# A graph layer pair on one core: shares in twos, chunk 5's sums in PSUM, edge bytes on ScalarE, eight tiles begun early

## The reference

```python
def _ggc(x, adj, W, wih, whh, bih, bhh):        # run twice, with relu around each
    m = adj @ (x @ W)
    gi, gh = m @ wih.T + bih, x @ whh.T + bhh
    r = sigmoid(i_r + h_r); z = sigmoid(i_z + h_z)
    n = tanh(i_n + r * h_n)
    return (1.0 - z) * n + z * x
x = layernorm(x + both gated layers)
# second layer: weights that depend on the rank of each edge in its row
support = x @ weight
mask = (adj != 0); rank = cumsum(mask, axis=1); deg = rank[:, -1:]
k = minimum(deg, 100); pos = rank - (deg - k)
w = mask * where(pos > 0, 0.5 ** (k - pos), 0)
x = layernorm(x + w @ support + bias)
```

## Time and profile before

| what | value |
|---|---|
| median of 3 runs | 375.72 us (375.42 to 377.91) |
| profiled execution | 376.38 us, its span 374.7 us |
| PE busy | 350.6 us, 94% |
| DVE busy | 301.1 us, 80% |
| ACT busy | 152.6 us, 41% |
| stream loads | 212 of 512 KB, 6.5 us from issue to landing |

### The profile page before, as it was taken

How to read it: one execution, slowest core, us unless ns; L and a number is a source line. 1 busy time by engine, 2 the same in 40 slices (tenths; PEclk the granted TensorE clock), 3 DMA queues, 4 the chain that set the end, 5 groups by cost and what they waited for, 6 DMA issues and landing times.

```text
span 374.7 us, 6469 instructions
## 1 busy us (share of the span) xinstructions
PE 350.6 (94%) x2424; PEld 156.1 (42%) x2424; DVE 301.1 (80%) x476; ACT 152.6 (41%) x185; POOL 25.6 (7%) x32
## 2 busy tenths in 40 slices
PE   4996979999999999999999899999999999969993
PEld 1431213333333333333333224444444453859992
DVE  1488978788886877889976498969896999888993
ACT  0003303022031210312103238758687868676992
POOL 1000000000000000000000020202020201102242
PEclk9999999999999999999999899999999999998998
DMA  7999999999999999999999999999999996100011
GB/s 232 405 393 389 409 380 408 372 409 366 401 409 365 393 318 407 356 356 335 348 378 329 385 352 390 350 352 343 349 360 369 374 357 242 30 0 4 2 58 58
DMA packets 36366, 117.38 MB, mean 313 GB/s; under 512 B 4208, under 2 KB 8560, under 8 KB 36336
## 3 DMA queue, kind: packets, MB, share of 16 engines
q1 hardware_dynamic: 36336, 116.97, 84.5%
HBM read 114.86 MB, written 1.05 MB: 309 GB/s over the span
## 4 chain that ended last, share of the span: by engine, by line
PE 70%; DMA 16%; ACT 6%; DVE 4%; issue 2%; POOL 1%; SPq 1%; POOLq 0%; DVEq 0%; ACTq 0%
PE m_acc L435 40%; DMA stream<-in_adj_t 14%; PE out L435 12%; PE out L540 6%; PE rz_ps L513 3%; PE rz_ps L499 2%; DMA hx<-in_x_pairs 2%; PE rz_ps L492 2%; ACT codes L690 2%; PE n_ps L492 2%; PE m_acc L467 1%; ACT s_mid L690 1%; ACT stream L690 1%; DVE codes L1022 1%; POOL rstd L781 1%
## 5 line engine op out<-in xcount | busy, mean ns | idle before, releaser
L435 PE MATMUL m_acc<-stream,s_in 128*64 128x512 f32 x512 | 127.7, 611 | 7.1 <-DMA stream<-in_adj_t 6.5
L840 DVE TENSOR_SCALAR codes<-stream 128x1024 uint8<-128x1024 f32 x128 | 83.8, 686 | 13.8 <-DMA stream<-in_adj_t 13.6
L435 PE MATMUL m_acc<-stream,s_mid 128*64 128x512 f32 x280 | 67.6, 604 | 0.8 <-DMA stream<-in_adj_t 0.7
L435 PEld LDWEIGHTS m_acc<-stream,s_in 128*64 128x64 f32 x512 | 33.2, 138 | 75.1 <-issue 48.9
L435 PE MATMUL out<-stream,s_mid 128*64 128x512 f32 x232 | 58.9, 598 | 0.4 <-DMA stream<-in_adj_t 0.4
L781 POOL TENSOR_TENSOR rstd<-var,mhalf 128x4 f32<-128x4 f32 x16 | 23.7, 1484 | 345.4 <-DVE var L990 345.4
L886 DVE SCALAR_TENSOR_TENSOR codes<-codes,run 128x1024 uint32<-128x1024 uint32 (+2 forms) x36 | 39.8, 1107 | 1.2
L881 DVE TENSOR_TENSOR run<-run,codes 128x2048 uint16<-128x2048 uint16 (+2 forms) x35 | 38.4, 1098 | 1.2
L690 ACT ACTIVATE wexp<-codes,code_bias 128x2048 uint16<-128x2048 uint8 x18 | 35.7, 1990 | 1.9 <-PE out L540 1.9
L622 ACT ACTIVATE m_high<-m_acc 64x512 f32<-64x512 f32 x14 | 8.3, 594 | 57.4 <-PE m_acc L435 47.2
L690 ACT ACTIVATE codes<-codes,code_bias 128x2048 uint16<-128x2048 uint8 x16 | 31.6, 1987 | 0.0
(11 more groups left out here) (148 smaller groups left out, 390.0 us busy)
## 6 DMA issues: line engine op xcount, KB each, us to landing
stream<-in_adj_t SPq DMA_DIRECT2D x212, 512.0 KB, 6.5
hx<-in_x_pairs SPq DMA_DIRECT2D x8, 128.0 KB, 7.7
mx<-in_x_t SPq DMA_DIRECT2D x8, 128.0 KB, 7.1
mx<-hx SPq DMA_DIRECT2D x16, 64.0 KB, 4.8
x_res<-in_x_pairs SPq DMA_DIRECT2D x8, 128.0 KB, 5.0
out_nodes<-stream SPq DMA_DIRECT2D x8, 128.0 KB, 1.9
const<-in_consts SPq DMA_DIRECT2D x1, 358.0 KB, 7.9
bias_b<-in_bias SPq DMA_DIRECT2D x1, 128.0 KB, 8.0
```

The source lines that it names most:

```text
L435: last = nc.tensor.matmul(to[D * u:D * (u + 1), :], state[:, t * D:(t + 1) * D], stream[:, n % SLOTS, u * CW:(u + 1) * CW], start=start[u] ...
L840: nc.vector.tensor_scalar(edges(p // 2, b, 2 * (p % 2), 2), stream[:, n % SLOTS, :], 0.0, None, ALU.not_equal).then_inc(mask_made, 1)
```

## The change

`TRI[6]` goes from 4 to 5: chunk 6 does ten pairs twice in pass 1 and, as chunk 7, leaves six for pass 2; its pairs, sums and needs take the order of chunk 7. Chunk 5 keeps its bank until pass 2, so `KEPT` ends at 4; for that `count_ps` becomes one bank. The shares stand at (0, 0, 3, 3), two before the first pair and two behind the node. ACT makes the bytes of five pairs of chunk 6 and six of chunk 7, with Sign to int8 and then Square to uint8. `CHAIN_EARLY` takes eight tiles, four in each of chunks 6 and 7, and the tiles of pass 2 are laid out anew: six in t=1, four in t=2 to 4, five in t=5 and 6, none in t=7.

```diff
-TRI = (0, 0, 2, 3, 4, 4, 4, 5)
-KEPT = range(2, 6)
+TRI = (0, 0, 2, 3, 4, 4, 5, 5)
+KEPT = range(2, 5)
+M2_BANK = {2: 2, 3: 1, 4: 2, 5: 3, 6: 1, 7: 2}
+M2_AFTER = {4: 2, 6: 3, 7: 4}
...
-NEED = [(8, 12, 16)] * 2 + [(8, 15, 16)] * 5 + [(8, 13, 16)]
+NEED = [(8, 12, 16)] * 2 + [(8, 15, 16)] * 4 + [(8, 13, 16)] * 2
-TURN = [(0, 10), (0, 11), (0, 12), (0, 13), (1, 8), (1, 9), (1, 10), (1, 11), (1, 12),
-        (0, 14), (0, 15)]
+TURN = [(0, 10), (0, 11), (0, 12), (0, 13), (1, 10), (1, 11), (1, 12), (0, 14), (0, 15),
+        (1, 13), (1, 14), (1, 15)]
...
-KEEP, KEEP_ADD = 9, 10
+KEEP, KEEP_ADD, GUARD_AT = 9, 10, 10
-CHAIN_EARLY = {6: {12: 1, 14: 1}, 7: {9: 1, 12: 1}}
+CHAIN_EARLY = {6: {10: 1, 11: 1, 12: 1, 14: 1}, 7: {5: 1, 8: 1, 10: 1, 12: 1}}
+BY_SIGN = {6: (8, 9, 11, 13, 14), 7: (1, 8, 9, 11, 13, 14)}
-ALONG_PAIRS = {1: 12, 2: 12, 3: 12, 4: 12, 5: 12, 6: 13}
+ALONG_PAIRS = {1: 11, 2: 12, 3: 12, 4: 12, 5: 12, 6: 11}
-SHARE_AT = {2: (0, 1, 4, 6), 3: (0, 1, 4, 6), 4: (0, 1, 4, 6), 5: (0, 1, 4, 6), 6: (0, 1, 4, 6)}
+SHARE_AT = {t: (0, 0, 3, 3) for t in range(2, 7)}
...
-CHAIN = [chain_tiles(*x) for x in ((0, 4), (4, 8), (8, 12), (12, 16), (16, 20), (20, 25), (25, 30),
-                                   (30, 32), (32, 32))]
+CHAIN = [chain_tiles(*x) for x in ((0, 4), (4, 10), (10, 14), (14, 18), (18, 22), (22, 27), (27, 32),
+                                   (32, 32), (32, 32))]
...
-        count_ps, spare_ps = out_ps[0:2], out_ps[3]
+        count_ps, spare_ps = out_ps[0], out_ps[3]
...
-                        sp.wait_ge(mask_made, n - SLOTS + 1)
+                        by_dve, by_sign = masks_before(n - SLOTS + 1)
+                        if signed(n - SLOTS):
+                            sp.wait_ge(signs_read, by_sign)
+                        else:
+                            sp.wait_ge(mask_made, by_dve)
...
-                if b >= 2:
-                    pe.wait_ge(start_made, b - 1)
+                if b >= 1:
+                    pe.wait_ge(start_made, b)
...
+            def sign_mask(b, q):
+                n, p = b * NP + q, PAIRS[b][q]
+                to = edges(p // 2, b, 2 * (p % 2), 2)
+                act.wait_ge(adj_in[n % SLOTS], 16 * (n // SLOTS + 1))
+                nc.scalar.activation(to.bitcast(I8), stream[:, n % SLOTS, :], ACT.Sign)\
+                    .then_inc(signs_read, 1)
+                act.wait_ge(signs_read, masks_before(n)[1] + 1)
+                nc.scalar.activation(to, to.bitcast(I8), ACT.Square).then_inc(squares_made, 1)
...
-                dve.wait_ge(mask_made, b * NP + NEED[b][part])
+                by_dve, by_sign = masks_before(b * NP + NEED[b][part])
+                dve.wait_ge(mask_made, by_dve)
+                if by_sign:
+                    dve.wait_ge(squares_made, by_sign)
```

More of the change, by code:

```diff
@@ L10 @@
 U16 = mybir.dt.uint16
+I8 = mybir.dt.int8
 I32 = mybir.dt.int32
@@ L54 @@
          [0, 8, 1, 9, 2, 10, 3, 11, 6, 12, 7, 13, 4, 14, 5, 15],
-         BY_TURNS, BY_TURNS, BY_TURNS,
-         [0, 10, 1, 11, 2, 12, 3, 13, 4, 14, 5, 6, 7, 15, 8, 9]]
+         BY_TURNS, BY_TURNS] + [[0, 10, 1, 11, 2, 12, 3, 13, 4, 14, 5, 6, 7, 15, 8, 9]] * 2
 QUADS = [(slice(0, 2), slice(2, 4), slice(4, 6), slice(6, 8))] * 2 + \
     [(slice(0, 4, 2), slice(4, 6), slice(1, 4, 2), slice(6, 8))] + \
-    [(slice(0, 2), slice(4, 6), slice(2, 4), slice(6, 8))] * 4 + \
-    [(slice(0, 2), slice(5, 7), slice(2, 4), slice(4, 8, 3))]
-NEED = [(8, 12, 16)] * 2 + [(8, 15, 16)] * 5 + [(8, 13, 16)]
-TURN = [(0, 10), (0, 11), (0, 12), (0, 13), (1, 8), (1, 9), (1, 10), (1, 11), (1, 12),
-        (0, 14), (0, 15)]
-LOADS = [(b, q) for b in range(NCH) for q in PAIRS[b]] + [(NCH + s, q) for s, q in TURN] + [(NCH + 1, q) for q in (13, 14, 15)] + \
+    [(slice(0, 2), slice(4, 6), slice(2, 4), slice(6, 8))] * 3 + \
+    [(slice(0, 2), slice(5, 7), slice(2, 4), slice(4, 8, 3))] * 2
+NEED = [(8, 12, 16)] * 2 + [(8, 15, 16)] * 4 + [(8, 13, 16)] * 2
+TURN = [(0, 10), (0, 11), (0, 12), (0, 13), (1, 10), (1, 11), (1, 12), (0, 14), (0, 15),
+        (1, 13), (1, 14), (1, 15)]
+LOADS = [(b, q) for b in range(NCH) for q in PAIRS[b]] + [(NCH + s, q) for s, q in TURN] + \
         [(NCH + s, q) for s in range(2, NCH) for q in range(2 * TRI[NCH - 1 - s], NP)]
@@ L152, with signed, masks_before @@
 OUT_ACT = (0, 2, 4)
+def signed(n):
+    return n % NP in BY_SIGN.get(n // NP, ())
+def masks_before(n):
+    by_sign = sum(signed(m) for m in range(n))
+    return n - by_sign, by_sign
 def tile_step(j, k):
@@ L244, in build @@
         out_ps = [ctx.enter_context(nc.psum_tensor(f"out{i}", [P, CW], F32)) for i in range(4)]
-        count_ps, spare_ps = out_ps[0:2], out_ps[3]
+        count_ps, spare_ps = out_ps[0], out_ps[3]
         end_ps = out_ps + [m_acc[0], m_acc[1], n_ps, rz_ps]
         def m2_bank(b):
-            return out_ps[2 + b % 2]
+            return out_ps[M2_BANK[b]]
         def acc_bank(g):
-            return m2_bank(2 * NCH - 1 - g) if g in (NCH, NCH + 1) else m_acc[g % 2]
+            return m2_bank(2 * NCH - 1 - g) if NCH <= g <= NCH + 2 else m_acc[g % 2]
         def kept_part(b):
@@ L448, in product1 @@
                     if first:
-                        if b == 3:
+                        if b == 5:
                             pe.wait_ge(to_sup_made, 4)
-                        if b - 2 in KEPT:
-                            pe.wait_ge(m2_kept, KEPT.index(b - 2) + 1)
+                        if b in M2_AFTER:
+                            pe.wait_ge(m2_kept, KEPT.index(M2_AFTER[b]) + 1)
                     last = pair(n, q, s_mid, m2_bank(b), [first] * 2, q == twice[-1] and b in KEPT)
@@ L458, in product2 @@
                 n = LOAD_AT[g, q]
-                first = s >= 2 and q == 2 * TRI[ch]
+                first = s >= 3 and q == 2 * TRI[ch]
                 pe.wait_ge(s_mid_made, q // 2 + 1)
                 if first:
-                    pe.wait_ge(m_ready, s + 5 if s < 4 else s + 7)
+                    pe.wait_ge(m_ready, {3: NCH, 4: NCH - 1}.get(s, s + 7))
                     if ch in KEPT:
@@ L525, in share @@
                 if first:
-                    if i < 2:
+                    if i == 0:
                         pe.wait_ge(start_made, NCH)
                     elif i < 4:
-                        pe.wait_ge(m_ready, NCH + 4 - i)
+                        pe.wait_ge(m_ready, NCH + (2, 1, 3)[i - 1])
                     elif i < 6:
@@ L598, in chunk2 @@
                         node(NCH + t - 1)
-                    if t >= 2 and n in SHARE_AT[t]:
-                        share(t - 2, SHARE_AT[t].index(n))
+                    for i in range(ALONG):
+                        if t >= 2 and n == SHARE_AT[t][i]:
+                            share(t - 2, i)
                     if n < ALONG_PAIRS[t]:
@@ L665, in start_run @@
                 act.wait_ge(count_done, b + 1)
-                nc.scalar.activation(run[0][:, bass.ts(b, CW)], count_ps[b % 2][:, :], ACT.Relu,
+                nc.scalar.activation(run[0][:, bass.ts(b, CW)], count_ps[:, :], ACT.Relu,
                                      bias=start_bias[:, :]).then_inc(start_made, 1)
@@ L712, in _ @@
                         keep_copy(b - 1)
+                    if signed(b * NP + q):
+                        sign_mask(b, q)
             high(NCH - 1)
@@ L944, in _ @@
                         combine(b - 1)
-                    mask(b, q)
+                    if not signed(b * NP + q):
+                        mask(b, q)
                     if b == 0 and q % 2 == 1 and q < NP - 1:
@@ L963, in _ @@
                             keep_add(b - 1)
-                    if b == EARLY and q == KEEP:
+                    if b == EARLY and q == GUARD_AT:
                         guard(False)
```

5 lines of the change are left out of this document (3 added, 2 removed).

## The result

The changed kernel takes 374.10 us (median of 15 runs, 372.16 to 376.18) against 375.88 for the kernel before (15 runs, 374.30 to 378.11): ratio 0.9944, 95% interval 0.9924 to 0.9964. By the ratio it is faster by 2.1 us (the medians are 1.8 us apart), which is clear of noise; 4.6 us were forecast, and 374.10 lies inside the forecast range of 367.3 to 375.0.

The account below looks back on a forecast made before the run. PE was taken to bound chunks 3 to 7 and most of pass 2, transfers its start. The terms, led by -3.75 (shares) and -3.0 (start), summed to -4.6 us: 375.72 becomes 371.1, range 367.3 to 375.0.

Parts of the forecast that it names:

- the shares in twos: Steps t=2 to 6: fewer entries and exits save PE 0.75 us each, -3.75 in all if PE sets the pace.
- the ring: Gates 9 to gates 13 (t=2 to 5); the shares in twos were to save 0.75 us in each step.
- the start: Gates 7 to gates 9, 30.65 us before: -3.0 us, limited by transfers at 393 GB/s.
- transfers bind: Rival (0.23): nine products in a row against seven slots lose 0.5 us in each of t=2 to 4; 374.1.
- What DVE gives back in t=1 and t=3: DVE's tiles make n_input(9) late in t=1, +0.6 us, and the sigmoid late in t=3, +1.2 us.
- Two pairs moved: Two products go from t=6 to chunk 6 of pass 1: +1.7 us in chunk 6, -1.7 in t=6.
- Node 14: Five tiles each in t=5 and 6 fill DVE; node 14 waits 2.5 us in place of 0.70: +1.8.
- Node 14 to 15: In t=7, without its two tiles, node 15 stands 12.3 us behind node 14 in place of 13.73: -1.45.
- Masks on ScalarE, eight early tiles: Pass 1: ScalarE's masks cost nothing and save DVE 7.5 us, which pays 7.6 us for four more tiles.
- Sign needed no table of its own: Rival (0.07): Sign needs another table set, with loads in chunks 6 and 7: +1.3 us, 372.4.
- gates 8 without a wait: Sign the forecast is right: at the start of pass 2 the 1.46 us wait for mx goes.
- node 11 has no wait: Sign the forecast is wrong: node 11 without a wait, where the late sigmoid in t=3 was to cost +1.2 us.

Follow-up runs that it names:

- run 1: Changed kernel with the shares back at (0, 1, 4, 6) in t=2 to 6: ratio to the kernel before 0.9957.
- run 2: Changed kernel with the second couple of shares three pairs later, at (0, 0, 6, 6): ratio to the kernel before 0.9970.
- run 6: Changed kernel, full loads, with one ScalarE expansion per step moved ahead of x1s in t=2 to 6: ratio to the kernel before 0.9957.
- run 8: Changed kernel with all 128 masks on DVE, the eight early tiles kept: ratio to the kernel before 0.9955.
- run 10: Changed kernel with the expansion moved ahead of x1s and the shares at (0, 0, 6, 6): ratio to the kernel before 1.0061.
- run 11: Changed kernel with the expansion moved ahead and pass 2 tiles at 6, 4, 4, 5, 5, 4 in t=1 to 6: ratio to before 0.9926.
- run 12: As run 11, with the second couple of shares at pair 6 in t=2 to 5 and pair 3 in t=6: ratio to before 0.9915.
- run 5: Changed kernel with second-pass loads halved and one ScalarE expansion per step moved ahead of x1s in t=2 to 6: one run, 367.67 us.
- run 4: Kernel before with every load of the second pass cut to half, 256 KB: ratio to the kernel before 0.9919.
- run 7: Kernel before with only the shares in twos, (0, 0, 3, 3): ratio to the kernel before 1.0003.
- Half loads: Every second-pass load cut to 256 KB in place of 512: changed kernel (run 3) 0.9849, kernel before (run 4) 0.9919.
- run 3: Changed kernel with every load of the second pass cut to half, 256 KB: ratio to the kernel before 0.9849.
- run 9: Loads in six slots of the stream in place of seven, against the changed kernel: one run, 381.93 us.

## Why the prediction was wrong

The direction was right and the profile, by chance, had the predicted difference (4.3 us for 4.6). The runs have 2.1. Two terms failed: the shares in twos, whose 3.0 us in the ring did not come because the sum let PE alone set the pace there, and the start, whose transfers did not run at 393 GB/s. Term by term, over the eight profiles with the changed TURN, seven slots and full loads (the changed kernel and runs 1, 2, 6, 8, 10, 11, 12):

- **Shares in twos, -3.75: right on PE, wrong on the time.** PE's saving was exact: its step is 16.8 us in run 5 and 17.57 in run 4. In t=6 it came (run 1: 0.96). In the ring it did not: 73.34 us before and after. Over the whole kernel run 7 gives 0 and run 1 gives 0.5. The sentence "if PE sets the pace" carried the term, and in t=2 to 5 PE does not: seven slots bring 12 loads in about 18.3 us, and the loop over DVE and ScalarE has 17.8. I had the loop's pieces in hand for single stalls and never held its sum against the new step. My rival, transfers bind, named the right engine and a time of 374.1, but that it hit the median is in part luck: it put the cause on nine products in a row, which runs 2, 10 and 12 speak against. And the argument against it compared with the old step: 372 GB/s over 17.60 us are 6.55 MB, and in 16.85 us these would need 389 GB/s, where t=3 to 5 of the changed kernel got 335 to 373.
- **Start of the second pass, -3.0.** The eight have 28.40 to 30.69 us, mean 29.7, against 30.65 and 29.91 in the two profiles with the old one. That is -0.6. Half loads show that PE had 2.8 us to gain. But I let all the bytes come at the 393 GB/s of the early stage. Between gates 8 and 9 the eight profiles come near it, 377 to 392 GB/s; between gates 7 and 8, where PE is busy for 11.4 to 11.9 us of 12.2 to 13.4, they have 331 to 344, and over the whole start 361 to 370, with which the 10.9 MB take 29 to 30 us. The profiled execution happened to have the fastest start of all eight, 28.40. The stall at gates 8 went (1.46 us in the earlier trace rows, none in the changed kernel), but the slow clock was no part of it that could be counted on: run 7 has the same stall of 1.46 us with the clock at 1.00, and its start is only 0.7 us shorter than the kernel before's.
- **What DVE gives back in t=1 and t=3, +0.6 and +1.2.** They are there when transfers are not: run 3 waits 1.18 us before node 9 and 1.19 before node 11. With full loads they lie behind the transfers: the changed kernel has neither wait.
- **Two pairs moved, +1.7 and -1.7.** Chunk 6 +1.72; t=6 went from 18.63 to 15.97, -2.66 with its share couple, -2.47 in the sum.
- **Node 14, +1.8.** 5.14 to 5.97, so +0.8; +0.8 to +1.7 in runs 1, 2, 3, 5, 6 and 8, which have the same tiles. Run 11 shows the cause.
- **Node 14 to 15, -1.45.** -2.14 where node 14 waited up to 1.82 us; only -0.5 where it waited 2.2 to 2.4 us (runs 2, 3, 5), as the clock fell.
- **Masks on ScalarE, eight early tiles.** The masks cost nothing, as reckoned, and gain nothing (run 8); DVE had room for them. The early tiles were never taken out by themselves; chunk 7 is as long as before (22.62 us for 22.61) and chunk 6 longer by its two products alone. Sign needed no table of its own: that rival fell.

With the measured terms: +1.7 - 0.6 + 0 - 2.7 + 0.8 - 2.1 = -2.9, and -2.1 measured for all runs. The 0.8 us between them is less than what single sections swing by.

Of the signs named beforehand, gates 8 without a wait and the full clock came true. So did two that were to show the forecast wrong: PE waits on `stream` before the last of the nine products, and node 11 has no wait. Node 14 waits 1.56 us where 2 to 3 were expected.

What stays open: why the transfers reach only 335 to 383 GB/s in the steps of the ring (309 in one of run 12), where early pass 1 has 393 with seven slots too. Depth matters (run 9); the order of the shares moves the waits but not their sum. Inside the steps of the changed kernel the rate swings more than that, while the DMA engines stay busy (shares of 1.03 and 0.98):

```profile
262.70:265.00 2.30, 2.30 (x31) 1.44 (x28) 0.76 (x1) 2.30 (x2) 0.00 (x0) 1.00 1.03 422
289.00:291.00 2.00, 2.00 (x26) 1.32 (x25) 1.97 (x4) 1.60 (x1) 0.78 (x1) 1.00 0.98 263
```

The low stretches, 271 to 273 us (275 GB/s) and 289 to 291 (263), come 3 to 5 us behind SP's issue of the next state's two `mx` loads of 64 KB, 267.67 and 285.93. That these small loads take engine time that the stream then lacks is a rival to slots alone as the cause; no run tests it. Single steps swing by 2 us from profile to profile, as t=4 in run 12, there in part by the clock.

## What to carry to other kernels

Before counting a saving on the busiest engine, add up every loop that returns to the same point of the next step (here h_c to h_c over DVE and ScalarE) and the rate at which the slots come back, and hold both against the new step, not the old one. A loop near the length of the old step shows no wait in the trace of before; it shows as time in hand that shrinks from step to step (1.37 and then 1.08 us here). Work that an engine has room for need not be moved: DVE was busy for 24.3 of 25.2 us and the chunk was no longer. And one profiled execution can be the fastest of its kernel, or the slowest, so place it among the runs before reading 2 us from it.

## What the runs showed of the hardware

- The granted clock fell to about half, from 2.4 to 1.2 GHz, right behind some waits of PE and not behind others. It fell behind 1.46 us for mx in the kernel before (0.55 from 208.12 to 210.85 us), 1.84 us on `stream` in run 12 (0.51), 2.2 to 2.4 us for node 14 in runs 2, 3 and 5, and 4.31 us in run 10. It stayed at 1.00 behind the same 1.46 us for mx in runs 4 and 7, 1.5 to 1.8 us for node 14 (changed kernel, runs 1, 6, 8) and 1.7 to 1.9 us on `stream` (runs 8 and 9). So up to 1.9 us these rows do not tell beforehand whether it falls. From node 14 to 15 it was 0.87 or 0.88 in runs 2, 3 and 5, which cost 1.6 us: 13.2 in place of 11.6.
- Square of 1024 int8 elements took 1.057 us, and Sign of 1024 f32 elements 1.043 us: reading one-byte data was not faster on ScalarE than reading f32.
- Taking one of seven slots cost the ring 4.1 us of 73.3, about 6%, and t=6 another 2.4 us (one run).
